# Flamingo-style gated attention and FFN on one core: fp16 halves straight into the value product, scores ahead of it

## The reference

```python
q = layernorm(x) @ Wq;  k = ctx @ Wk;  v = ctx @ Wv        # 16 heads of 64
dots = where(mask | causal, -max, einsum('bhid,bhjd->bhij', q, k) / 8)
out = einsum('bhij,bhjd->bhid', softmax(dots), v)
x = x + tanh(g_xattn) * (out @ Wo + bo)
x = x + tanh(g_ffn) * ffn(layernorm(x))   # 4-bit weights, activations rounded to 16 bits
```

## Time and profile before

| | |
|---|---|
| median of 3 runs | 1627.03 us (1625.19 to 1629.18) |
| profiled execution, its own time | 1626.47 us |
| its span in the trace | 1624.6 us |
| mean granted TensorE clock | 0.982 of full speed |
| busy: PE, DVE, ACT, POOL | 94%, 85%, 77%, 64% of the span |

### The profile page before, as it was taken

How to read it: one execution, slowest core, us unless ns; L and a number is a source line. 1 busy time by engine, 2 the same in 40 slices (tenths; PEclk the granted TensorE clock), 3 DMA queues, 4 the chain that set the end, 5 groups by cost and what they waited for, 6 DMA issues and landing times. The chain is left out here.

```text
span 1624.6 us, 38058 instructions
## 1 busy us (share of the span) xinstructions
PE 1530.6 (94%) x12556; PEld 1251.8 (77%) x12556; DVE 1385.1 (85%) x2247; ACT 1253.4 (77%) x3222; POOL 1033.8 (64%) x1004
## 2 busy tenths in 40 slices
PE   7899999999999999999999999789989997995998
PEld 5787887877877878878778788677767776775887
DVE  7888888888888888888888889878887998998996
ACT  5887887888778778878887787566758998885674
POOL 3988988888888889888888888600006664740000
PEclk9999999999999999999999999999998999997999
DMA  6554445444444544454444445369957884755664
GB/s 195 118 127 103 105 106 122 104 92 115 106 105 103 126 102 105 107 121 104 92 115 106 105 103 98 86 205 344 321 215 262 282 287 153 276 227 187 218 214 145
DMA packets 347365, 252.23 MB, mean 155 GB/s; under 512 B 287792, under 2 KB 317616, under 8 KB 344368
## 3 DMA queue, kind: packets, MB, share of 16 engines
q1 hardware_dynamic: 347312, 251.58, 55.1%
HBM read 105.25 MB, written 76.02 MB: 112 GB/s over the span
## 5 line engine op out<-in xcount | busy, mean ns | idle before, releaser
L496 ACT ACTIVATE prob<-masked,neg_max 128x128 f32<-128x128 f32 x1024 | 397.6, 391 | 35.1 <-DVE neg_max L662 31.6
L431 POOL TENSOR_TENSOR prob_parts<-prob,prob_parts 128x512 f16<-128x512 f32 x254 | 310.3, 1241 | 2.7 <-ACT prob_parts L504 1.6
L426 POOL TENSOR_TENSOR prob<-prob,scaled 128x512 f32<-128x512 f32 x256 | 271.6, 1061 | 20.1
L660 DVE TENSOR_TENSOR masked<-score,mask_add 128x512 f32<-128x512 f32 x256 | 174.6, 682 | 74.0 <-PE score L963 67.9
L504 ACT ACTIVATE prob_parts<-prob 128x512 f16<-128x512 f32 x254 | 159.0, 627 | 75.6 <-POOL prob L426 71.7
L496 ACT ACTIVATION_READ_ACCUMULATOR prob<-masked,neg_max 128x1 f32 x1024 | 193.3, 189 | 0.0
L662 DVE TENSOR_REDUCE neg_max<-masked 128x4 f32<-128x512 f32 x256 | 175.6, 686 | 8.8
L438 POOL TENSOR_TENSOR probT<-turn 128x512 f32<-128x512 f16 x125 | 173.2, 1386 | 0.0
L1723 POOL TENSOR_SCALAR xThi<-n_x 128x1024 fp32r<-128x1024 int16 x15 | 43.8, 2919 | 202.9 <-DMA n_x<-n_x_d 166.8
L976 PE MATMUL y<-wo_hi,o_hi 128*128 128x256 f32 x508 | 148.3, 292 | 15.9 <-DVE o_lo L667 15.2
L424 POOL TENSOR_TENSOR scaled<-rsums,pscale 128x4 f32<-128x4 f32 x256 | 66.4, 259 | 124.0 <-DVE rsums L654 123.9
(11 more groups left out here) (249 smaller groups left out, 4485.5 us busy)
## 6 DMA issues: line engine op xcount, KB each, us to landing
gate<-gate_d SPq DMA_DIRECT2D x30, 768.0 KB, 4.3
n_x<-n_x_d SPq DMA_DIRECT2D x25, 512.0 KB, 4.9
gate_d<-stage SPq DMA_DIRECT2D x8, 1536.0 KB, 5.5
n_u_d<-w_raw SPq DMA_DIRECT2D x16, 768.0 KB, 4.1
stage<-n_u_d SPq DMA_DIRECT2D x16, 768.0 KB, 6.0
gate_d<-gate SPq DMA_DIRECT2D x7, 1536.0 KB, 5.5
x_in<-in_x SPq DMA_DIRECT2D x16, 512.0 KB, 3.9
ctx_in<-in_ctx_columns SPq DMA_DIRECT2D x16, 512.0 KB, 4.8
```

The lines of the kernel that those rows point to most:

```text
L426: gp.tensor_tensor(prob[:, h], prob[:, h], scaled[:, h, :].rearrange("p (b o) -> p b o", o=1).broadcast_to([P, NB, P]), ALU.mult).then_inc ...
L431: gp.tensor_tensor(prob_parts[:, h, 1], prob[:, h].rearrange("p b k -> p (b k)"), prob_parts[:, h, 0], ALU.subtract).then_inc(prob_low, 1)
L496: nc.scalar.activation(prob[:, h, b, :], masked[:, h, b, :], ACT.Exp, bias=neg_max[:, h, b:b + 1], accum_out=psums[:, h, b:b + 1]).then_in ...
L660: nc.vector.tensor_tensor(masked[:, h], score[h][:], mask_add[:], ALU.add).then_inc(masked_done, 1)
```

## The change

The turned halves are no longer added. v is kept in fp16 as well, as a high and a low half of v scaled by one number per group (v16), and times_v makes three fp16 passes: high by high, high by low, low by high, 24 matmuls a step in place of 8. join_prob and join_second go. ScalarE makes the high half of all eight value products (copy with the scale v_mul), then VectorE the low half of all eight (values). The scale comes from a bound on |v|: w_top, the maxima of |Wv| per row, once; c_top, the maxima of |ctx|, in c=6 (ctx_top); their product on TensorE in c=7 (value_bound); two small operations on VectorE at the end of c=7 (value_scale). It is taken out again in the residual, through y_unit (c=4). For the last unit, which TensorE turns itself, the halves are made by ScalarE and VectorE. In each step TensorE now does the scores first and times_v last; the DMA transpose into turn waits for the value product of two units back in place of the join.

```diff
-            def join_second(u, slot, times):
-                gp.wait_ge(prob_turned[1][slot], 16 * times)
-                wait(gp, pv_done, u)
-                gp.tensor_tensor(probT[:, 1], turn[:, slot, 1, 0:NB], turn[:, slot, 1, NB:2 * NB],
-                                 ALU.add).then_inc(probT_copied[1], 1)
...
-                if new and c > 2:
+                if new:
                     for i, n in jobs_of(c, "v"):
                         b, before = nth(g, i)
+                        if n == 0:
+                            act.wait_ge(v_scaled, 4 * g + 3)
                         act.wait_ge(projected[b], before + 1)
-                        nc.scalar.activation(v_sb[:, n % NB, VH:2 * VH], proj[b][:], ACT.Copy).then_inc(copied[b], 1)
+                        nc.scalar.activation(v16[:, n % NB, n // NB, 0], proj[b][:], ACT.Copy, scale=v_mul[:, 0:1]).then_inc(v_high, 1)
...
             def values(g, c):
                 for i, n in jobs_of(c, "v"):
                     b, before = nth(g, i)
-                    dve.wait_ge(projected[b], before + 1)
-                    nc.vector.tensor_copy(v_sb[:, n % NB, 0:VH], proj[b][:]).then_inc(copied[b], 1)
+                    dve.wait_ge(v_high, NC * g + n + 1)
+                    nc.vector.scalar_tensor_tensor(v16[:, n % NB, n // NB, 1], proj[b][:], v_mul[:, 0:1], v16[:, n % NB, n // NB, 0],
+                                                   ALU.mult, ALU.subtract).then_inc(copied[b], 1)
+            def ctx_top(g):
+                dve.wait_ge(ctx_loaded, 16 * (g + 1))
+                nc.vector.tensor_reduce(c_top[:], ctx_in[:], X, ALU.max, apply_absolute_value=True).then_inc(v_scaled, 1)
+            def value_scale(g):
+                dve.wait_ge(v_bound, g + 1)
+                nc.vector.tensor_scalar(v_unit[:], trans[:, 0, 0:1], 1.0 / VMAX, VTINY, ALU.mult, ALU.max).then_inc(v_scaled, 1)
+                dve.wait_ge(v_scaled, 4 * g + 2)
+                nc.vector.reciprocal(v_mul[:], v_unit[:]).then_inc(v_scaled, 1)
+                dve.wait_ge(v_scaled, 4 * g + 3)
...
-                if old:
-                    join_prob(u - 3, 0, (c + 1) % 2, NC // 2 * g + (c - 1) // 2)
...
+                if c == 4:
+                    output_unit(g)
+                if c == 6 and more:
+                    ctx_top(g + 1)
...
-                if c < 3:
-                    values(g, c)
+                values(g, c)
+                if nxt:
+                    value_scale(g + 1)
...
+            dve.wait_ge(w_loaded[5], 16)
+            nc.vector.tensor_reduce(w_top[:], w_stage(2), X, ALU.max, apply_absolute_value=True)
+            ctx_top(0)
             w_low_part(3)
...
-                    for h in range(2):
-                        last = nc.tensor.matmul(pv[h * HD:(h + 1) * HD, b, :], v_sb[:, b, c * P + h * HD:c * P + (h + 1) * HD],
-                                                probT[:, h, b, :], start=True, stop=True)
+                    for n, (m, t) in enumerate(((0, 0), (0, 1), (1, 0))):
+                        for h in range(2):
+                            at = c % NB * P + h * HD
+                            last = nc.tensor.matmul(pv[h * HD:(h + 1) * HD, b, :], v16[:, b, c // NB, m, at:at + HD],
+                                                    turn[:, slot, h, t * NB + b, :], start=(n == 0), stop=(n == 2))
                 last.then_inc(pv_done, 1)
+            def value_bound(g):
+                pe.wait_ge(v_scaled, 4 * g + 1)
+                for k in range(KC):
+                    last = nc.tensor.matmul(trans[:, 0, 0:1], c_top[:, k:k + 1].broadcast_to([P, P]), w_top[:, k:k + 1],
+                                            start=(k == 0), stop=(k == KC - 1))
+                last.then_inc(v_bound, 1)
...
+                if new:
+                    scores_free(g, c, u)
+                    pe.nop(nofuse=True)
+                    scores(g, c, u)
                 if old:
-                    times_v(u - 3, co, (g, c, u) if new else None)
-                if new:
-                    if not old:
-                        scores_free(g, c, u)
-                    scores(g, c, u)
+                    times_v(u - 3, co, (c + 1) % 2, NC // 2 * g + (c - 1) // 2)
```

More of the change, by code:

```diff
@@ L130, in attention @@
         kT = sb("kT", [P, T])
-        v_sb = sb("v_sb", [P, NB, INNER])
+        v16 = sb("v16", [P, NB, 2, 2, VH], F16)
+        v_stage = v16[:].rearrange("p b h n i -> p (b h n i)").bitcast(F32).rearrange("p (b i) -> p b i", b=NB)
+        w_top, c_top = sb("w_top", [P, KC]), sb("c_top", [P, KC])
+        v_unit, v_mul, y_unit = (sb(n, [P, 1]) for n in ("v_unit", "v_mul", "y_unit"))
         masked = sb("masked", [P, 2, NB, P])
@@ L202, in attention @@
         xres_loaded = sem("xres_loaded")
-        probT_copied = [sem(f"probT_copied{h}") for h in range(2)]
+        v_high = sem("v_high")
+        v_scaled = sem("v_scaled")
+        v_bound = sem("v_bound")
+        last_turned = sem("last_turned")
         pv_done = sem("pv_done")
@@ L573, in _ @@
             attended(U - 2)
-            act.wait_ge(last_step, 1)
             act.wait_ge(pv_done, U - 1)
-            nc.scalar.activation(probT[:, 0], trans[:], ACT.Copy).then_inc(probT_copied[0], 1)
-            for n in range(4):
+            for h in range(2):
+                act.wait_ge(last_step, h + 1)
+                nc.scalar.activation(turn[:, 1, h, 0:NB], trans[:], ACT.Copy).then_inc(v_high, 1)
+                if h == 0:
+                    ffn_high_part(0)
+            for n in range(1, 4):
                 ffn_high_part(n)
@@ L642, in w_low_half @@
                     last.then_inc(w_ready, 1)
[L644 to L649, removed]
             def reciprocals(u, h):
@@ L723, in step @@
                         work(*args)
+                if isinstance(g, int) and u == 0:
+                    value_scale(0)
                 if soft:
                     reciprocals(u - 1, 1)
-                if c < 3:
-                    values(g, c)
+                values(g, c)
+                if nxt:
+                    value_scale(g + 1)
                 if c == 4 and after_first:
@@ L847, in _ @@
             attended_low(U - 3)
-            for h in range(2):
-                join_prob(U - 2, h, 0, U // 2)
             attended_low(U - 2)
             weight_values(2, 1)
-            ffn_low_part(0)
-            dve.wait_ge(last_step, 2)
-            dve.wait_ge(pv_done, U - 1)
-            nc.vector.tensor_copy(probT[:, 1], trans[:]).then_inc(probT_copied[1], 1)
+            for h in range(2):
+                dve.wait_ge(v_high, NC * G + h + 1)
+                nc.vector.tensor_tensor(turn[:, 1, h, NB:2 * NB], trans[:], turn[:, 1, h, 0:NB], ALU.subtract).then_inc(last_turned, 1)
+                if h == 0:
+                    ffn_low_part(0)
             for n in range(1, 4):
@@ L937, in scores_free, with times_v @@
                     wait(pe, masked_done, 2 * (u - 1) + h + 1)
-            def times_v(u, c, then=None):
+            def times_v(u, c, slot, times, then=None):
                 for h in range(2):
-                    pe.wait_ge(probT_copied[h], u + 1)
+                    if times is None:
+                        pe.wait_ge(last_turned, 2)
+                    else:
+                        pe.wait_ge(prob_turned[h][slot], 16 * times)
                 wait(pe, out_split, u)
@@ L996, in step @@
                     weights_left(g, c, jobs_of(c, "k")[0][0], 1)
+                if first:
+                    value_bound(0)
                 if nxt:
@@ L1006, in step @@
                     transpose_in(g, *ts[1])
+                    value_bound(g + 1)
                 if first or fourth:
```

41 lines of the change are left out of this document (20 added, 21 removed).

## The result

The changed kernel takes 1688.78 us (median of 4 runs, 1682.06 to 1691.93) against 1626.13 us before on the same chip: 1.0376 times as long, 95% interval 1.034 to 1.0413. The forecast was slower, 1667 us within 1606 to 1690: the sign was right, the size was 22 us short, and the median lies only 1.2 us inside the range, with two of the four runs above it. The profiled execution took 1691.93 us, span 1690.2.

The account below looks back on a forecast made before the run. TensorE was taken to bound the attention part. +2.5 us a group times 15 (+37), about +4 at the start and -1 at the end made +40 on a median of 1627.0: 1667 us, range 1606 to 1690.

Parts of the forecast that it names:

- The value product: In each step, 24 fp16 matmuls take 0.83 us where the f32 product took 1.02, a gain of 0.19 us.
- the rival that loads bind: Weight loads make the value product 1.45 us instead of 0.83: +3.7 us a group, 1723 us; chance 0.08.
- The order and the joins: In each step, the value product's result lands about 0.6 us later but covered; dropping two probT sums gains nothing on the path.
- c=5: TensorE's output product waits 2.0 us more, as VectorE's small layer-norm operations take turns with GpSimd's low halves; bounds 0 and 2.4.
- its sign: Output product of c=5 about 5 us into the step, released by o_lo; v_eps, vare or m_dif near 1 us.
- c=6 and c=7: c=6 0.3 us longer; c=7 1.2 us longer, normalising being held in GpSimd's run and the second transpose late.
- The start: w_top and ctx_top come before VectorE's weight halves, and the first value halves wait for the scale: about +4 us.
- The bounds of c=5 and c=7: Extra time in c=5 between 0 and 2.4 us, in c=7 between 0.2 and 1.9; said to give 1640 to 1690 us.
- the rival in which every wait goes: Today's waits in c=5, c=0 and c=7, 2.0 us in all, vanish: -3.2 us a group, 1578 us; chance 0.07.
- The rival that operations are not held: VectorE's operations behind the value half in c=4 and c=6 pass GpSimd's: -0.8 us a group, 1617 us; chance 0.27.

Follow-up runs that it names:

- the mended kernel: Changed kernel with nothing but its half of v ending VectorE's steps: layer-norm work moved to other steps on VectorE and GpSimd, ctx_top to c=5; 1598.31 us, 0.9829.
- the moves: Layer-norm work moved to other steps on VectorE and GpSimd; on the kernel before, without the change: 1643.55 us, or 1628.02 us with GpSimd's xres sum in c=1.

## Why the prediction came out as it did

*The value product: right, a little larger.* 24 records start within 0.79 us of the next query product (forecast 0.83), c=1 to c=4 are at 7.37 (7.43). Over eight steps that is half a microsecond a group more than forecast, and it hides half of what the clock costs below. The 24 weight loads of 64 columns fit into the 0.79 us, in pairs that start every 0.056 us: the rival that loads bind (1723 us) is out. The Trainium skill ("TensorE: Matmul & The Clock Gate", LDWEIGHTS) gives columns / 1.2 in ns for a load; by an estimate from that, 24 loads one behind another take 1.28 us. The trace agrees with it only if the two loads of a pair overlap.

*The order and the joins: right.* The order alone is 1.0011, and on the mended kernel it is nothing either. That the joins taken out gained nothing, as costed, no run shows by itself; with the moves the traces speak for the room that they leave.

*c=5: the wait right, its consequence missed.* The forecast put m_sum at T+7.6 and the masked sum at T5+3.0, the output product near T5+5.07; measured T+7.24, T5+2.88, T5+4.95. The number of turns was right, though which of the operations are held was not: v_sum and mean (1.13 and 1.15 us), while v_eps, vare and m_dif, which the forecast named as its sign, took 0.16, 0.17 and 0.15. The step that failed is the next one, "so TensorE waits 2.0 us more": it counts the wait and keeps the lengths of the matmuls behind it. Where the granted clock falls to 0.50, c=5 takes 1.6 us more (11.1 against 9.5). In the run that kept TensorE at work the clock stayed at 1.00, and a group is 1.1 us shorter; that is nearly all of the 1.2 us by which the group was mis-sized.

*c=6 and c=7: right in mechanism, 0.2 and 0.5 us short.* The masked sum behind x_in's normalising begins at T7+3.23 (forecast T7+3.0), and with GpSimd's low halves cut short the normalising takes half the time. The second transposes come at T7+6.85 (forecast 6.6), just as the key copy ends; but the output product ahead of them, which waits 1.19 us for o_lo, ends at the same moment, so this lateness had two ways to TensorE and not one. A clock fall in two of the groups makes 0.2 of the 0.5.

*The start: the mechanism right, the size 9.9 us instead of 4.* w_top and c_top take 3.5 us, as costed, but w_top also waits 1.02 us for its load, so that TensorE stands still for 4.46 us until c_top is there and the first step takes 13.9 us instead of 9.4. In the next steps v needs ScalarE's copy, queued behind weight halves of 1.05 and 1.89 us, and then VectorE's, so that TensorE waits for it in steps in which it did not before. The clock at 0.50 belongs to the picture, but it does not set the size: in the run that kept TensorE at work it fell for 6.8 us instead of 13.7, and the second group began at 88.40, no earlier. Of the terms of the sum this was the second that was mis-sized.

*What is left.* The profiled run is 65.6 us longer than that of before: 9.9 at the start, 52.3 in groups 1 to 14, 0.4 less from the last group to the last output product, and 3.6 behind it. The forecast had 4 at the start, 2.5 for each of 15 groups, and 1 less at the end, so the last group was counted in full although no net loss occurs there. The part behind attention, which the change does not touch, takes 565.4 to 574.0 us in the profiled runs, so its 3.6 us are scatter.

*The range and the rivals' prices.* The upper end, 1690, is not what the working gives. The bounds of c=5 and c=7 that it names lie 0.4 and 0.7 us above the terms of the sum, 16.5 us in 15 groups, which makes 1684; the lower bounds, 2.0 and 1.0 below, make 1622 and not 1640. The measured 1688.78 is above what these bounds allow, since the fall of the clock and most of the start are in none of them: that it lies inside the range is luck. In the rival in which every wait goes, transposes of 0.66 us leave 0.3 us of waits in c=7 and not 0.8, which makes 1587 us and not 1578.

The rival that operations are not held (1617 us) is what the run with short low halves in two steps made true, 1620.31 us. In the trace v_sum and mean take 1.13 and 1.15 us beside low halves, and the maximum c_top takes 1.19 us with GpSimd at work nearly all the while and 1.21 with nothing beside it. The Trainium skill ("SBUF — State Buffer", Who interferes with whom) says that a VectorE instruction with two SBUF inputs, or in a two-port mode, and a GpSimd instruction that reads SBUF shut each other out for a whole instruction, while a reduction is not concerned. The trace agrees for v_sum, with two inputs, and for the maximum; mean has one, and that it runs in a two-port mode no run here shows.

## What to carry to other kernels

Before an instruction is put into a queue, look at what is pushed back and what runs on the neighbouring engine at the new time: seven operations of 0.15 us cost TensorE a wait of 1.9 us, because they came to stand beside GpSimd's long instructions. Price a wait of TensorE not by its length alone but also by the rows behind it, whose clock may have fallen. And when a change slows a kernel, mend the queue before dropping the change: here each half of the mended kernel was worth nothing or less alone, and both together 1.7%.

## What was not expected of the hardware

At c=5 TensorE stood still for 1.93 us in all of the groups 1 to 14, and in 11 of them the granted clock then went from 1.00 to 0.50. It fell between the end of the wait and 1.5 us later, when TensorE was already at work again; here is the latest, in a group whose output product starts at 875.69 (windows):

```profile
875.70:877.15 1.45, 1.45 (x12) 1.45 (x13) 1.42 (x4) 1.45 (x8) 0.03 (x1) 1.00 0.17 31
877.25:878.70 1.45, 1.45 (x5) 1.16 (x5) 0.41 (x2) 1.45 (x8) 1.24 (x2) 0.50 0.00 0
```

With 12 transposes that nothing reads in the wait, it never fell there. With c=5's wait gone and c=7's left (short low halves in c=4), it fell in c=7 in 8 of 14 groups (10.85 us against 9.40). Why it falls in one group and not in another with the same wait was seen but not taken apart.
